# A decoder layer on one core: the in-projection by seven block products in place of eight, its output halves and running sum through DRAM

## What is computed

```python
# mixer (Mamba-2 style), then x = _layernorm(x + mixer(x))
h = x * jax.lax.rsqrt(jnp.mean(x * x, axis=-1, keepdims=True) + EPS) * norm_w
proj = jnp.einsum('bsd,od->bso', h, in_proj_w)
gate = proj[..., :D_INNER]                               # D_INNER = 8192
hBC = proj[..., D_INNER:D_INNER + CONV_DIM]              # hid 8192, B 1024, C 1024
dt = proj[..., D_INNER + CONV_DIM:]                      # 128 heads
hBC = jax.nn.silu(causal_conv(hBC, conv_w, conv_b))      # 4 taps along the tokens
...
y = (Y_diag + Y_off).reshape(b, S, H_M, P_M)[:, :s] + D_res
yg = y * jax.nn.silu(gate)
ygr = yg.reshape(b, s, G_M, gsz)                         # 8 groups of 1024 channels
ygr = ygr * jax.lax.rsqrt(jnp.mean(ygr * ygr, axis=-1, keepdims=True) + EPS)
out = jnp.einsum('bsd,od->bso', ygr.reshape(b, s, D_INNER) * gnorm_w, out_proj_w)
return residual + out
# then cross-attention over the context, _layernorm, a feed-forward layer with a
# top-2 router over 8 low-rank experts, _layernorm
```

## Time and profile before

| what | before |
|---|---|
| median of 3 runs (lowest, highest) | 1453.74 us (1453.47, 1454.0) |
| span of the profiled execution | 1451.6 us |
| busy: TensorE, VectorE | 98%, 68% of the span |
| busy: ScalarE, GpSimd | 52%, 35% of the span |
| chain that ended last, TensorE's share | 89% (L1231 46%, L1298 20%) |
| one group, from second half to second half | 144.55 us |

### The profile page before, as it was taken

One profiled execution on the slowest core, in us unless ns is written; L12 is line 12 of the kernel. 1 busy time (PEld: TensorE's weight loads), 2 busy tenths in 40 slices (PEclk: granted clock), 3 DMA queues, 4 the chain that ended last, 5 costly groups with the idle time before them and its releaser, 6 DMA issues.

```text
span 1451.6 us, 29769 instructions
## 1 busy us (share of the span) xinstructions
PE 1417.7 (98%) x12610; PEld 1161.2 (80%) x12610; DVE 988.1 (68%) x1304; ACT 759.0 (52%) x1022; POOL 505.2 (35%) x374
## 2 busy tenths in 40 slices
PE   6999999999999999999999999999999999999996
PEld 5888989898989898989898989888988865545552
DVE  5784768476847684768476847684768397888764
ACT  6774637463756375637463746374637345553340
POOL 5252425242524252425242534153415322111101
PEclk9999999999999999999999999999999999999998
DMA  5431213131312131213121312131212158466610
GB/s 167 124 107 43 89 50 100 50 90 41 100 54 87 41 100 58 85 40 98 59 88 39 100 55 88 41 100 54 87 41 89 66 219 331 188 234 265 196 54 13
DMA packets 53407, 142.59 MB, mean 98 GB/s; under 512 B 9782, under 2 KB 9910, under 8 KB 47012
## 3 DMA queue, kind: packets, MB, share of 16 engines
q1 hardware_dynamic: 51604, 137.13, 28.9%
q0 software_dynamic: 1600, 3.44, 0.7%
q10 hardware_dynamic: 70, 0.11, 0.0%
HBM read 136.53 MB, written 2.29 MB: 96 GB/s over the span
## 4 chain that ended last, share of the span: by engine, by line
PE 89%; DVE 5%; ACT 2%; issue 1%; POOL 1%; DMA 0%; SPq 0%; DVEq 0%; POOLq 0%; ACTq 0%
PE bank L1231 46%; PE bank L1298 20%; PE bank L1539 6%; PE bank L1454 5%; PE bank L1275 4%; PE bank L1262 4%; PE bank L1511 2%; DVE conv L863 1%; ACT qT L757 1%; PE bank L1525 1%; DVE decay L922 1%; PE bank L1507 1%; PE bank L1285 1%; PE bank L1519 1%; DVE keysT L990 0%
## 5 line engine op out<-in xcount | busy, mean ns | idle before, releaser
L1231 PE MATMUL bank<-h_hi,w_hi 128*128 128x448 f32 x1152 | 337.6, 374 | 2.7 <-DVE conv L863 2.1
L437 POOL TENSOR_TENSOR y_lo<-yg,y_hi 128x896 fp32r<-128x896 f32 x63 | 134.2, 2131 | 582.5 <-ACT y_hi L621 542.4
L1231 PE MATMUL bank<-h_lo,w_hi 128*128 128x448 f32 x1152 | 327.4, 365 | 0.0
L1231 PE MATMUL bank<-h_hi,w_lo 128*128 128x448 f32 x1152 | 326.9, 365 | 0.0
L863 DVE SCALAR_TENSOR_TENSOR conv<-bank,conv_w,conv 128x880 f32<-128x880 f32 (+2 forms) x240 | 268.0, 1117 | 84.9 <-ACT conv L594 79.2
L1231 PEld LDWEIGHTS bank<-h_hi,w_lo 128*128 128x128 f32 x1152 | 216.4, 188 | 17.5
L1231 PEld LDWEIGHTS bank<-h_lo,w_hi 128*128 128x128 f32 x1152 | 216.4, 188 | 17.1
L420 POOL TENSOR_TENSOR w_lo<-w_raw,w_hi 128x512 fp32r<-128x512 f32 x144 | 187.0, 1299 | 109.4 <-ACT w_hi L561 108.1
L1231 PEld LDWEIGHTS bank<-h_hi,w_hi 128*128 128x128 f32 x1152 | 207.9, 188 | 20.7 <-DVE conv L863 2.6
L910 DVE TENSOR_TENSOR hd_dt<-bank,dt_j 128x512 f32<-128x512 f32 x128 | 82.4, 685 | 203.3 <-PE bank L1262 202.9
L621 ACT ACTIVATE y_hi<-yg 128x896 fp32r<-128x896 f32 x64 | 60.9, 951 | 200.4 <-DVE yg L890 200.1
(11 more groups left out here) (184 smaller groups left out, 1910.1 us busy)
## 6 DMA issues: line engine op xcount, KB each, us to landing
w_raw<-in_w_in SPq DMA_DIRECT2D x144, 256.0 KB, 2.9
decay<-cs_scratch SPq DMA_DIRECT2D x128, 196.0 KB
ring_a<-in_context SPq DMA_DIRECT2D x24, 1024.0 KB, 7.4
ring_b<-in_context SPq DMA_DIRECT2D x21, 1024.0 KB
wo_raw<-in_w_out SPq DMA_DIRECT2D x64, 256.0 KB, 2.7
ring_b<-in_context SPq DMA_DIRECT2D x3, 896.0 KB
acc<-in_x SPq DMA_DIRECT2D x1, 1792.0 KB, 8.6
out<-z POOLq DMA_DIRECT2D x14, 112.0 KB, 3.8
```

The lines of the kernel that those rows point to most:

```text
L437: g_.tensor_tensor(y_lo[:, c % 4, :], yg[:, c % 2, :], y_hi[:, c % 4, :].bitcast(f32), ALU.subtract).then_inc(s["y_low"], 1)
L1231: last = mm(place, w[:, k * P:(k + 1) * P], x[:, k, half * HALF:(half + 1) * HALF], start=(k == 0 and i == 0), stop=(k == KT - 1 and i == 2))
```

## The change

**Seven products for eight.** Two weight tiles, a hidden and a gate tile of the same step (or B and C), are now treated as one. Cut into two halves of rows, two halves of the 512 features and two halves of the 896 tokens, their product would be 8 block products, each of 6 matmuls. The form of Strassen and Winograd needs 7 (`product1` to `product7`, 42 matmuls where 48 stood), and sums of blocks before and after. The sums of tokens' blocks (`t1` to `t4`) are made once. The sums of weight blocks are made on POOL for every pair of tiles: two of 256 columns (`sums_12`) and one of 512 (`sums_34`), and POOL also makes the low parts of all the factors: three of 512 (`low_wa`, `low_w13`, `low_w4`) and one of 256 (`low_ws2`). The high parts are copies on ACT. The results are put together out of PSUM and SBUF: ACT copies what must be kept (`keep_r1`, `keep_r2`, `keep_r3`, 448 wide) and DVE adds (`sum_c11`, `sum_c12`, `sum_c22`, 448 wide). The hidden product thus ends up in a tile `xh` in SBUF, and the convolution's taps (`tap`) read it there; C's taps (`taps_c`) read `cmat` in SBUF.

**Periods for steps.** A group is 9 periods n (k = n mod 9): k=0 is B and C, k=1 to 8 the steps. A `plain` period has one pair of tiles. In the lumps, k=7 (`first_lump`) and k=2 (`second_lump`, of the group before), the 7 token tiles of an out-projection half stand between block products, and the differences, exps and weighings for 4 channel tiles are done together.

**y is split for one token tile at a time:** 14 times 128x512 on ACT and POOL in a group, where 8 times 128x896 stood.

**Halves and running sum in DRAM.** SP stores each evacuated first half, reads it back for the second half, reads the running sum, and stores it again (`store_part`, `load_part`, `load_acc`, `store_acc`), through four 128x512 places in SBUF (`stream`).

A group's instructions that matter later, counted on either side: DVE with two tensor inputs in SBUF: 30 taps (before: none, its taps read PSUM), 8 gate products, 8 differences, 8 weighings, 8 `wo_low`, 7 `add_output` (all as before). POOL: 36 of 512 and 27 of 256 for the weights (before: 18 of 512), 7 additions of squares of 896 (as before), 14 `y_low` of 512 (before: 8 of 896), one group norm.

```diff
+            def store_part(g, t):
+                sp.wait_ge(s["evac_done"], TT * g + t + 1)
+                sp.dma_start(part_dram[t], stream[:, t % 2, :]).then_inc(part_stored[t % 2], 16)
...
+            def load_acc(g, t):
+                p = t % 2
+                at_least(sp, acc_stored[p], 16 * (SIDE[p] * g + t // 2))
+                sp.dma_start(stream[:, 2 + p, :], acc_dram[t] if g else x[:, t, :]).then_inc(acc_loaded[p], 16)
...
+            def store_acc(g, t):
+                sp.wait_ge(s["sum_done"], TT * g + t + 1)
+                sp.dma_start(acc_dram[t], stream[:, 2 + t % 2, :]).then_inc(acc_stored[t % 2], 16)
...
-                g_.tensor_tensor(y_lo[:, c % 4, :], yg[:, c % 2, :], y_hi[:, c % 4, :].bitcast(f32),
-                                 ALU.subtract).then_inc(s["y_low"], 1)
...
+            def sums_12(m):
+                    return
...
+                g_.tensor_tensor(w[:, 2, :], w[:, 3, :], w[:, 5, :], ALU.add).then_inc(s["s12_set"], 1)
...
+                g_.tensor_tensor(w[:, 4, :], w[:, 2, :], w[:, 0, :], ALU.subtract).then_inc(s["s12_set"], 1)
...
+            def low_ws2(m):
+                pool.wait_ge(s["ws2_high"], m + 1)
+                g_.tensor_tensor(ws2_lo[:], wr[m % 2][:, 4, :], ws2_hi[:].bitcast(f32),
+                                 ALU.subtract).then_inc(s["ws2_low"], 1)
...
+            def sums_34(m):
+                pool.wait_ge(s["ws2_low"], m + 1)
+                g_.tensor_tensor(w[:, 3:5, :], w[:, 0:2, :], w[:, 3:5, :], ALU.subtract).then_inc(s["s34_set"], 1)
...
+            def low_w13(m):
+                pool.wait_ge(s["w13_high"], m + 1)
+                g_.tensor_tensor(w13_lo[:], wr[m % 2][:, 2:4, :].rearrange("p a n -> p (a n)"),
+                                 w13_hi[:].bitcast(f32), ALU.subtract).then_inc(s["w13_low"], 1)
...
+            def low_w4(m):
+                pool.wait_ge(s["w4_high"], m + 1)
+                g_.tensor_tensor(w4_lo[:], wr[m % 2][:, 4:6, :].rearrange("p a n -> p (a n)"),
+                                 w4_hi[:].bitcast(f32), ALU.subtract).then_inc(s["w4_low"], 1)
...
+            def y_low(m):
+                i = m % (2 * TT)
+                first, t = (0, i) if i < TT else (1, i - TT)
+                pool.wait_ge(s["y_high"], m + 1)
+                g_.tensor_tensor(ysp_lo[:, m % 2], yg[:, first:first + 4, t * P:(t + 1) * P],
+                                 ysp_hi[:, m % 2].bitcast(f32), ALU.subtract).then_inc(s["y_low"], 1)
...
-                    else:
-                        wait(dve, s["conv_tap"], 30, g, 3 * m + sh - 1)
-                    v.scalar_tensor_tensor(out=dst[:, :, sh:LEN], in0=src[:, :, 0:LEN - sh],
-                                           scalar=conv_w[:, bass.ds(col, 1), TAPS - 1 - sh],
-                                           in1=dst[:, :, sh:LEN], op0=ALU.mult,
-                                           op1=ALU.add).then_inc(s["conv_tap"], 1)
...
+            def sum_c12(n):
+                dve.wait_ge(s["p3_done"], n + 1)
+                dve.wait_ge(s["r2_set"], n + 1)
+                v.tensor_tensor(xh[:, n % 2, HALF:TOK], wb, xh[:, n % 2, HALF:TOK], ALU.add).then_inc(s["c12_set"], 1)
...
+            def tap(n, sh):
...
+                v.scalar_tensor_tensor(out=dst[:, :, sh:LEN], in0=src[:, :, 0:LEN - sh],
+                                       scalar=conv_w[:, col, TAPS - 1 - sh:TAPS - sh], in1=dst[:, :, sh:LEN],
+                                       op0=ALU.mult, op1=ALU.add).then_inc(s["conv_tap"], 1)
...
-            def product(out, hi, lo, as_scaled=False):
-                for k in range(KT):
...
-                    for i, (w, x) in enumerate(((hi, h_hi), (hi, h_lo), (lo, h_hi))):
-                        for half in range(2):
-                            place = out[:, half, :].rearrange("p (b i) -> p b i", i=PAD)[:, :, 0:LEN]
-                            last = mm(place, w[:, k * P:(k + 1) * P],
-                                      x[:, k, half * HALF:(half + 1) * HALF],
-                                      start=(k == 0 and i == 0), stop=(k == KT - 1 and i == 2))
...
+            def block_product(out, w, at, x, start, stop):
+                (w_hi, w_lo), (x_hi, x_lo) = w, x
+                for k in range(2):
+                    cols = slice(at + k * P, at + (k + 1) * P)
+                    for i, (wt, xt) in enumerate(((w_hi, x_hi), (w_hi, x_lo), (w_lo, x_hi))):
+                        last = mm(out, wt[:, cols], xt[:, k, :], start=(start and k == 0 and i == 0),
+                                  stop=(stop and k == 1 and i == 2), skip_group_check=True)
...
+            def product2(m):
+                at_least(pe, s["c11_set"], m)
+                block_product(zb, wa, 256, b21, True, True).then_inc(s["p2_done"], 1)
...
+            def product6(m):
+                pe.wait_ge(s["ws2_low"], m + 1)
+                pe.wait_ge(s["r1_set"], m + 1)
+                block_product(yb(m), ws2, 0, t2, False, False).then_inc(s["p6_done"], 1)
...
+            def product3(m):
+                pe.wait_ge(s["w4_low"], m + 1)
+                pe.wait_ge(s["c22_set"], m + 1)
+                block_product(wb, w4, 0, b22, False, True).then_inc(s["p3_done"], 1)
...
-            def second_half(g):
...
-                sum_squares(g)
-                for t in range(TT):
-                    if t == 1:
-                        wait(pe, s["ss_picked"], 1, g, 0)
-                    elif t > 1:
-                        wait(pe, s["psum_added"], TT, g, t - 1 - TT)
-                    out_product(t, (t + 1) % 2, g, 0).then_inc(s["outb_done"], 1)
...
+            def out_product(m, b):
+                pe.wait_ge(s["y_low"], m + 1)
+                for c in range(4):
+                    for i, (y, w) in enumerate(((ysp_hi, wo_hi), (ysp_hi, wo_lo), (ysp_lo, wo_hi))):
+                        last = mm(ob[:, b, :], y[:, m % 2, c, :], w[:, c, :], start=(c == 0 and i == 0),
+                                  stop=(c == 3 and i == 2))
...
+            def second_lump(n):
+                g = n // STEP
+                product7(n)
+                product5(n)
+                second_out(g - 1, 0)
+                sum_squares(g - 1)
+                product1(n + 1)
+                second_out(g - 1, 1)
+                product2(n + 1)
+                cb_product(g)
+                second_out(g - 1, 2)
+                product3(n)
+                second_out(g - 1, 3)
+                product6(n + 1)
+                second_out(g - 1, 4)
+                product4(n)
+                second_out(g - 1, 5)
+                transpose_hid(chan(n - 1))
+                second_out(g - 1, 6)
...
+            def plain(n):
+                product7(n)
...
+                product5(n)
+                product1(n + 1)
+                product2(n + 1)
+                y_product(chan(n - 2))
...
+                product3(n)
+                product6(n + 1)
...
+                product4(n)
+                transpose_hid(chan(n - 1))
```

More of the change, by code:

```diff
@@ L321, in _ @@
[L321 to L340 removed]
+            load_tile1(1)
@@ L401, in _ @@
             for q in range(2):
[L402 to L404 removed]
+                g_.tensor_copy(spread[:, PAD * q:PAD * q + LEN], ident[:, LEN * q:LEN * (q + 1)])
+            for slot in range(4):
+                g_.memset(decay[slot][:], 0.0)
             g_.memset(bmat[:], 0.0)
@@ new lines, in _, with y_high_last @@
+            for n in range(NP - 1):
+                if n % STEP == 7:
+                    first_lump(n)
+                elif n % STEP == 2 and n > 2:
+                    second_lump(n)
+                else:
+                    plain(n)
+            def y_high_last(i, hi, before):
+                act.wait_ge(s["g_done"], CHANS - 3 + i)
+                act.wait_ge(s[before], NP)
+                a(hi[:].rearrange("p k n -> p (k n)"), yg[:, 4 - i, :], ACT.Copy).then_inc(s["ylast_high"], 1)
@@ new lines, in from_turned @@
+            def from_turned(out, b, half, other, diff):
+                for k in range(2):
+                    dve.wait_ge(s["hT_done"], KT * half + 2 * b + k + 1)
+                    if k == 0 and diff:
+                        dve.wait_ge(s["x_diff"], diff)
+                    last = v.scalar_tensor_tensor(out=out[:, k, :], in0=turned(b, half, k), scalar=weight(b, k),
+                                                  in1=other[:, k, :], op0=ALU.mult, op1=ALU.subtract)
+                return last
@@ new lines, in _ @@
+            sum_c11(0)
+            for n in range(NP - 1):
+                if n % STEP == 7:
+                    first_lump(n)
+                elif n % STEP == 2 and n > 2:
+                    second_lump(n)
+                else:
+                    plain(n)
+            scale_hid(CHANS - 3)
+            tap(NP - 2, 1)
+            sum_c22(NP - 1)
+            tap(NP - 2, 2)
+            tap(NP - 2, 3)
+            add_skip(CHANS - 3)
+            multiply_gate(CHANS - 3)
+            sum_c12(NP - 1)
```

1652 lines of the change are left out of this document (1034 added, 618 removed).

## The result

The changed kernel takes 1661.79 us (median of 4 runs, 1656.31 to 1664.13) where the kernel before, measured beside it, takes 1453.61 (1453.32 to 1454.0): slower, ratio 1.1423 with a 95% interval of 1.1401 to 1.1445. The forecast had the direction and its cause, with 1575 and a range to 1640; the size is 87 us off.

A forecast was written before the change was run, and what follows sets the result against it. VectorE and GpSimd excluding each other on two-SBUF-input instructions binds the groups: 7 x 14 + 26 - 7.4 + 7 = 123.3 on the 1451.6 span, plus 2.1, 1577, stated as 1575. Range 1495 to 1635, stretched 1480 to 1640.

The forecast's parts named there:

- TensorE's 133.6 a group: TensorE's time per group after losing 54 matmuls of 0.2025 us, down from 144.55; a plain period 10.5, a lump 30.
- Two inputs in SBUF bring the taps into the exclusion: Taps reading two SBUF inputs cannot overlap GpSimd's instructions; VectorE and GpSimd together then need 148.4 us a group; chance 0.85.
- The price of a turn: Time past the other engine's end: 0.94 for a tap on VectorE, 1.15 for GpSimd's 512 columns.
- The plain periods: Seven periods a group, bound by VectorE's and GpSimd's summed need, 12.7 us in a usual one against TensorE's 10.5: 95.4.
- outside the exclusion: VectorE's own load per group, put at 117 us, below TensorE's 133.6 and so not the bound.
- The lumps' 60 on TensorE cover theirs: In the lumps, TensorE's 60 us a group cover the 53 that VectorE and GpSimd need for y_low and weighings.
- The 3 us that I added: Allowance in the second lump, where y_low of k=1 spills over: 155.4 a group becomes 158.5.
- Start: First out-projection product at 135 us instead of 109.15, +26: 101.5 without waits, 23 of ScalarE waits, 10 for the exclusion.
- End: After the last group: -7.4 from a shorter lump and period, +7 for a VectorE key part and sums from DRAM.
- Free taps: Rival: taps escape the exclusion, TensorE binds the groups, total 1409 us; chance 0.12.
- The slow passage through DRAM: Rival with free taps: storing and reloading token tiles' sums costs 8.5 us a group in the second lump, 1451; chance 0.03.
- A clock that falls in the gaps: Named danger to the forecast size: TensorE's clock may drop in idle gaps, which the earlier kernel's groups lack; no size given.

The follow-up runs named there:

- all four kinds freed and the two moves: Changed kernel with VectorE's taps, gate products, differences and weighings as one-SBUF-input reductions, k=0 out-projection weights loaded earlier, and norm squares before the first difference: 1459.52 us.
- the run on the end: Changed kernel with weights loaded earlier and squares before the first difference, plus the second context unit's key part on VectorE moved behind the last norm's statistics: 1654.78 us.
- the taps really freed: Changed kernel with each convolution tap a VectorE reduction over the same columns, one SBUF input instead of two: 1542.72 us, ratio 1.0604.
- the one with the two moves: Changed kernel with k=0 out-projection weights loaded ahead of in-projection loads, and norm squares and first half-sum ahead of the second lump's first difference: 1650.67 us.

## Why the prediction was right in cause and wrong in size

**TensorE's 133.6 a group**: 3 us too low. With all four kinds freed and the two moves TensorE is busy 136.6 us a group (956.32 / 7, in the window below) at clock 0.99, the plain period comes to 10.70 (10.5 reckoned) and the first lump to 30.0 (30); a group still takes 139.4.

**Two inputs in SBUF bring the taps into the exclusion**: right, shown from both sides. With one input they take 1.05 beside the same GpSimd work and 119 us go; given two, the kernel before loses 147, with GpSimd's list as it was. The price of a turn (0.94 after GpSimd's end, 1.15 after VectorE's) held in the changed kernel, with 0.93 and 1.16. No run took GpSimd's added work away, or let the taps of the changed kernel read PSUM, so how the loss divides between the taps' new place and the longer list isn't shown.

**The plain periods**: right in number by luck, since the reason doesn't hold. The 95.4 for seven of them less the 19.9 of k=1 is 75.5; measured are 52.6 + 23.9, less the last token tile of the second lump (2.7, at the head of k=3), 73.8. But this was a sum of need, and the run with y_lo and squares on VectorE lowered the need by 15 us a group and took 0.9 off it. What is nearly full is VectorE's queue. I put VectorE at 117 us a group "outside the exclusion" and so not the bound; in the trace it is busy 147.1 of 167.1 (sum of the four windows), and 780.63 / 7 = 111.5 a group with all four kinds freed and the two moves:

```profile
133.80:1117.60 983.80, 956.32 (x8135) 826.69 (x8135) 780.63 (x974) 708.87 (x1107) 721.28 (x603) 0.99 0.40 125
```

The difference of 36 us is, but for the 2 or 3 by which the reductions are shorter, its waits for GpSimd, and they stand in an in-order queue ahead of the additions out of PSUM that TensorE needs. That this queue sets the plain period is read from these traces; no run shortened it and left the exclusion as it was.

**"The lumps' 60 on TensorE cover theirs"**: this is the step that failed. Lumps and k=1 were put at 19.9 + 60 + 3 = 82.9 and take 33.9 + 55.6 + 2.7 = 92.2. The sum spreads the lumps' need of 53 evenly over them. In the kernel a lump's first products wait for y_lo, at the end of the list that GpSimd brings along from k=6 or k=1, which need 15 and 20 against TensorE's 10.5; the chain above is that list. In the second lump the next product waits 3.9 for the squares behind two taps and a difference. TensorE's surplus comes after all this, when nothing is left for it to cover. The 3 us that I added were 12: 9.3 more, and with the plain periods 1.7 less, that is, but for rounding, the 7.4 by which these six groups exceed 158.5. With the longer first group the seven make 59 of the 87 us. TensorE's lower clock isn't the cause: with its gaps filled the group still takes 165.0.

**Start**: 135 forecast, 150.0 measured, and the term that was too low is TensorE's own time, not its waits. From TensorE's start at 17.75 us, the changed kernel and the one with all four kinds freed and the two moves:

```profile
17.75:150.00 132.25, 99.00 (x709) 83.76 (x708) 97.96 (x95) 77.45 (x122) 89.27 (x63) 0.91 0.22 64
17.75:133.80 116.05, 93.26 (x708) 80.69 (x708) 77.12 (x95) 77.43 (x122) 72.60 (x63) 0.96 0.26 73
```

TensorE is idle for 33.25 us in the first, where the sum had 23 + 10, and for 22.8 in the second, where it had 23 without the exclusion; its longest wait, for a gate, is 11.6 and 9.1. But it is busy for 99.0 and 93.3, where 71.7 + 12 = 83.7 was put at full clock. In the first the lower clock explains at most 12 of these 15 us; this is an estimate: a mean of 0.91 means the half level for 0.18 x 132 = 24 us, in which half the work gets done. What the clock does cost there is open, since no run filled the gaps of the start.

**End**: the +7 and -7.4 came out as +11.8 and -3.3. What follows the groups took 64.7 and 265.9 in the kernel before:

```profile
1121.00:1185.74 64.74, 64.55 (x498) 54.11 (x498) 39.31 (x52) 24.21 (x31) 16.64 (x12) 1.00 0.30 111
1185.74:1451.60 265.86, 248.35 (x2804) 127.17 (x2804) 199.94 (x380) 112.13 (x207) 44.83 (x73) 0.98 0.51 188
```

The 64.7 became 73.2, and 68.9 with all four kinds freed and the moves. In the 73.2 TensorE works 61.21, at clock 0.94, and is idle for 12.0 where it was for 0.2. The transfers of the run on the end lie on the chain there, but no run took them away, so their share stays open. The attention behind takes 270.1 in place of 265.9 (270.2 in that same freed kernel). TensorE is idle no longer there (17.2 against 17.5) but busy for 4.5 more, at clock 0.96 where it had 0.98; why is open.

**The rivals.** Free taps were to give 1409; the taps really freed give 1543, since 24 other VectorE instructions and the order of the queues hold the groups as well. Even with these freed and the two moves the kernel only draws level, 1459.5 to 1454: 7 x 4.0 us saved in the groups of the profiled execution (983.8 / 7 = 140.5), 25 lost at the start and 8.5 behind the groups. The slow passage through DRAM, 8.5 us a group, didn't come about: VectorE waits 0.6 us in all for a running sum in the groups (and 12.6 in 7 waits ahead of the same instruction whose release the profile doesn't show, so 1.9 a group at most), and a store of 256 KB lands in 2.0 to 2.3 us. A clock that falls in the gaps was named as a danger; it fell, and filling the gaps of the groups gave back 4 us.

No version here that leaves nothing out beats the kernel before; the best of them is the one with the two moves, 1650.67.

## What to carry to other kernels

Before moving a source of VectorE from PSUM into SBUF, look what GpSimd does at that time: two SBUF inputs made a tap of 1.11 us one of 1.8 to 2.1. The sum of both engines' needs against the period is only a lower bound. Each turn is a wait in an in-order queue, so ask which instruction stands behind it and who is waiting for that; a kernel with VectorE busy 68% and GpSimd 35% of its span lost 10% in this way. Where TensorE is the bound, its waits needn't be the whole price: in that kernel they made 106 of the 147 us, and TensorE was busy for 44 longer. And where a stage is costed by its own bound, a lump between stages is costed by what its first instruction waits for, not by its sum.

## What I had not expected of the hardware

A VectorE reduction over the same 848 to 880 columns of an SBUF source runs beside GpSimd without any delay (1.05 us with and without one beside it), in place of 1.80 for the operation with two sources. And an instruction of GpSimd can be held as much as VectorE's: its additions of squares, 2.13 us before, have a mean of 2.80 in the changed kernel and 2.12 when the taps have one input.
